# Row maxima of an attention layer from three of six products, two heads at a time in the two halves of TensorE's rows

## The reference

```python
q = qkv[..., :nH * d].reshape(B, S, nH, d)
k = qkv[..., nH * d:nH * d + d]
v = qkv[..., nH * d + d:]
scores = jnp.einsum('bqhd,bkd->bhqk', q, k) * scale
alibi = slopes[:, None, None] * (pos_k - pos_q).astype(jnp.float32)
scores = jnp.where(causal[None, None], scores + alibi[None], NEG_INF)
probs = jax.nn.softmax(scores, axis=-1)
attn = jnp.einsum('bhqk,bkd->bqhd', probs, v).reshape(B, S, H)
return attn @ Wo
```

## Time and profile before

| | |
|---|---|
| Time, median of 3 runs | 1293.03 us (1291.48 to 1293.97) |
| The profiled execution, time | 1289.91 us |
| The profiled execution, span of the trace | 1288.1 us |
| PE busy (matmul) | 1170.8 us, 91% |
| DVE busy | 715.8 us, 56% |
| ACT busy | 583.2 us, 45% |
| Mean granted TensorE clock | 0.977 of full speed |

### The profile page before, as it was taken

One profiled execution on the slowest core, in us unless ns is written; L12 is line 12 of the kernel. 1 busy time (PEld: TensorE's weight loads), 2 busy tenths in 40 slices (PEclk: granted clock), 3 DMA queues, 4 the chain that ended last, 5 costly groups with the idle time before them and its releaser, 6 DMA issues. The chain is left out here.

```text
span 1288.1 us, 16700 instructions
## 1 busy us (share of the span) xinstructions
PE 1170.8 (91%) x6137; PEld 715.2 (56%) x6208; DVE 715.8 (56%) x1374; ACT 583.2 (45%) x1047; POOL 338.5 (26%) x366
## 2 busy tenths in 40 slices
PE   4879999999989999999998799999999999299995
PEld 4535534543543433344535577788788787256663
DVE  4378598688678897788713643331421300655654
ACT  5425456465547677857574443211111111134443
POOL 1214114112220231211034554111211111115554
PEclk9989999999989999999999999999999999699998
DMA  4451502400140420303120222300200100500304
GB/s 157 97 83 55 94 18 42 108 17 18 29 87 1 107 34 18 75 18 67 28 99 26 73 66 87 107 22 1 98 1 1 66 1 1 150 28 5 126 0 130
DMA packets 71567, 72.15 MB, mean 56 GB/s; under 512 B 39826, under 2 KB 45226, under 8 KB 71468
## 3 DMA queue, kind: packets, MB, share of 16 engines
q1 hardware_dynamic: 67284, 60.35, 18.8%
q0 software_dynamic: 3152, 8.63, 2.1%
q10 hardware_dynamic: 1056, 2.16, 0.5%
HBM read 51.86 MB, written 18.87 MB: 55 GB/s over the span
## 5 line engine op out<-in xcount | busy, mean ns | idle before, releaser
L1125 DVE TENSOR_REDUCE mx<-bank 128x1 f32<-128x512 f32 (+2 forms) x576 | 364.6, 684 | 98.5 <-PE bank L1317 54.7
L1048 ACT ACTIVATE PT<-ST 128x512 f32<-128x512 f32 x576 | 311.4, 600 | 106.4 <-PE ST L1393 62.4
L1314 PE MATMUL bank<-KS,QS 125*128 125x512 bf16 (+2 forms) x896 | 204.1, 309 | 12.5 <-DMA QS<-q_scratch 4.2
L1393 PE MATMUL ST<-QS,KS 128*128 128x512 bf16 x527 | 185.0, 383 | 9.1 <-DMA QS<-mparts 3.3
L1407 PE MATMUL PO<-PT,V 128*32 128x512 f32 x1152 | 152.8, 604 | 1.4 <-ACT PT L1048 1.0
L1694 DVE TENSOR_TENSOR f_h<-f_h,f_pair 128x512 f32<-128x512 f32 (+1 forms) x44 | 30.2, 687 | 207.5 <-ACT f_h L1643 207.5
L1314 PEld LDWEIGHTS bank<-KS,QS 125*128 125x128 bf16 x896 | 78.5, 99 | 113.3 <-DVE mx L1125 33.5
L56 PE MATMUL f_pair<-f_xT,gw 128*128 128x512 f32 (+1 forms) x352 | 140.0, 398 | 0.0
L58 PE MATMUL f_pair<-f_xT,gw 128*128 128x512 f32 (+1 forms) x352 | 137.9, 392 | 0.0
L57 PE MATMUL f_pair<-f_xT,gw 128*128 128x512 f32 (+1 forms) x352 | 137.9, 392 | 0.0
L1643 ACT ACTIVATE f_h<-f_pair 128x512 f32<-128x512 f32 (+1 forms) x44 | 26.3, 598 | 218.9 <-PE f_pair L58 218.8
(11 more groups left out here) (208 smaller groups left out, 1806.6 us busy)
## 6 DMA issues: line engine op xcount, KB each, us to landing
QS<-q_scratch SPq DMA_DIRECT2D x96, 128.0 KB
l_x<-x_dram SPq DMA_DIRECT2D x12, 512.0 KB, 4.1
q_scratch<-QP SPq DMA_DIRECT2D x36, 128.0 KB, 1.9
xres<-_attn_hidden_states_dram POOLq DMA_DIRECT2D x16, 256.0 KB, 3.1
x_dram<-xout POOLq DMA_DIRECT2D x16, 256.0 KB, 2.4
xin<-x_dram SPq DMA_DIRECT2D x4, 1024.0 KB, 7.6
f_xsum<-x_dram SPq DMA_DIRECT2D x4, 1024.0 KB, 7.2
x_dram<-f_xsum SPq DMA_DIRECT2D x4, 1024.0 KB, 4.6
```

Source lines behind the costliest of these rows:

```text
L1048: act.activation(PT[:, quad % PT_RING, n % 4, :], ST[:, n % ST_RING, :], ACT.Exp).then_inc(p_done, 1)
L1125: v.tensor_reduce(mx[:, i % 2, z, h:h + m], at(u).rearrange("p (m k) -> p m k", m=m), AX.X, ALU.max).then_inc(bank_free_dve, 1)
L1314: last = pe.matmul(at(u)[:, j * w:(j + 1) * w], QS[0:ROWS1, slot, h + j, :], KS[b][0:ROWS1, k0:k0 + w], start=(j == 0 or not diag), stop=( ...
L1393: last = pe.matmul(dst, KS[b][0:ROWS2, kb * P:(kb + 1) * P], QS[0:ROWS2, slot, h:h + 4, :], start=True, stop=not diag)
```

## The change

Only three of the six products go into the maxima (high with high, high with middle, middle with high). `Q_PART` and `K_PART` are reordered so that these three come first. The 128 rows of `QS` now consist of two halves of 64. For the first 16 heads the upper half holds the first three products, the six position rows and the three rows of the maxima (48 + 6 + 3), and the lower half the other three products; for the last 16 heads the halves are exchanged. So for each batch there are two arrangements of the keys, `KS[b][0]` and `KS[b][1]`, the second copied from the first by two DMAs for each piece (`swap_keys`). The second pass still contracts over all 128 rows.

A unit `p1` now makes two banks: head h in rows 0 to 53 and head h + 16 in rows 64 to 117, by alternate matmuls that write to neighbouring banks. The mask is then added to each bank by a matmul of its own, with the moving operand repeated by a stride of zero. DVE reduces both banks in one instruction of 1024 elements. There are 288 such units. Since a pair must not wrap round the ring, the planner leaves out a bank (`skipped`) where one would. The planner's cost of a unit is 240 ns on PE (218 before, for one bank) and 1130 ns on DVE (690 before, for one bank).

The stack of a block is twelve DMAs of half the size instead of six; the maxima go in by six DMAs instead of three; the position rows and key rows are loaded by more DMAs at the start. `keys_done` is two instructions for a piece instead of one.

```diff
@@ -32,12 +32,16 @@
 PARTS = 3
-Q_PART = (0, 0, 0, 1, 1, 2)
-K_PART = (0, 1, 2, 0, 1, 0)
+
+
+
+Q_PART = (0, 0, 1, 0, 1, 2)
+K_PART = (0, 1, 0, 2, 1, 0)
 SETS = len(Q_PART)
-POS = slice(SETS * HD, SETS * HD + 2 * PARTS)
-ROWS1 = P - PARTS
+ROWS1 = SETS // 2 * HD + 2 * PARTS
 ROWS2 = P
+HALVES = (0, P // 2)
+V_AT = P // 2 - HD
 QSLOTS = 4
 AHEAD = 2
...
@@ -181,7 +185,24 @@
 def maxima_of(i):
-    return [("p1", i, z, h) for z, (_, w, _) in enumerate(segments(BLOCKS[i][1])) for h in range(0, NH, 512 // w)]
+    return [("p1", i, z, h) for z, (_, w, _) in enumerate(segments(BLOCKS[i][1])) for h in range(0, NH // 2, 512 // w)]
+
+
+def banks_of(u):
+
+    return 2 if u[0] == "p1" else 1
+
+
+def skipped(n, count):
+
+    return int(count == 2 and n % RING == RING - 1)
+
+
+def take_banks(taken, u):
+
+    if skipped(len(taken), banks_of(u)):
+        taken.append(taken[len(taken) - RING])
+    taken.extend([u] * banks_of(u))
...
@@ -220,7 +241,7 @@
-    took = {"dt": 400, "dv": 520, "ds": 300, "p1": 218, "tile": 218, "pv": 1060, "xt": 400, "q": 700, "kv": 700, "vt": 400, "mt": 200, "ot": 400, "at": 400, "wo": 700}
+    took = {"dt": 400, "dv": 520, "ds": 300, "p1": 240, "tile": 218, "pv": 1060, "xt": 400, "q": 700, "kv": 700, "vt": 400, "mt": 200, "ot": 400, "at": 400, "wo": 700}
     reads = {"pe": 280, "act": 270, "dve": 270, "pool": 200, "sp": 0}
     free = {"pe": 0, "act": 0, "dve": 0, "pool": 0, "sp": 0}
...
@@ -283,7 +307,7 @@
     def pe_choices():
         out = []
-        dve_load = free["dve"] + sum(690 for j, r in pend["dve"] if r <= free["pe"] + 300)
+        dve_load = free["dve"] + sum(1130 if j[0] == "p1" else 690 for j, r in pend["dve"] if r <= free["pe"] + 300)
         act_load = free["act"] + sum(600 for j, r in pend["act"] if r <= free["pe"] + 300)
         if at["p1"] < len(p1):
...
@@ -478,7 +502,7 @@
                 end["xt", j[1], j[2]] = done
             elif kind == "kv3":
-                end["ks", j[1]] = done
+                sp_issue(("swap", j[1]), done)
             elif kind == "vt":
                 end["v", j[1]] = done
...
@@ -684,15 +708,15 @@
         kvf2 = sb("kvf", [P, 2, HALF])
         kvf = kvf2[:, 0, :]
-        mask = sb("mask", [P, 2, 512], BF16)
+        mask = sb("mask", [P, 2, P], BF16)
         gmask = sb("gmask", [P, 3])
         wo_s = [sb(f"wo{i}", [P, DC, D]) for i in range(2)]
         moments = sb("moments", [P, 4, 2])
         rstd = sb("rstd", [P, 4])
-        kpart = sb("kpart", [SETS * HD, 2, HALF], BF16)
-        krest = sb("krest", [SETS * HD, HALF])
-        KS = [sb(f"KS{b}", [P, S], BF16) for b in range(B)]
+        krest = kvf2[0:V_AT + P // 2, 1, :]
+        kpart = sb("kpart", [V_AT + P // 2, 2, HALF], BF16)
+        KS = [[sb(f"KS{b}{t}", [P, S], BF16) for t in range(2)] for b in range(B)]
         V = [sb(f"V{b}", [P, QB, 32]) for b in range(B)]
         gf = sb("d_gf", [P, DQ_COLS])
...
@@ -775,6 +800,10 @@
             return bank[:, AT[u] % RING, :]
+        def both(u):
+
+            return bank[:, AT[u] % RING:AT[u] % RING + 2, :]
+
         def full(eng, u):
...
@@ -837,20 +867,31 @@
                                  QP[:, part, m, cols_of(k)].rearrange("p (t q) -> p t q", q=P)).then_inc(q_out, 16)
+            def swap_keys(k):
+                b, t, n = PIECES[k]
+                sp.wait_ge(ks_ready, 2 * k + 2)
+                for x in range(2):
+                    sp.dma_start(KS[b][1][HALVES[1 - x]:HALVES[1 - x] + V_AT, t * P:(t + n) * P],
+                                 KS[b][0][HALVES[x]:HALVES[x] + V_AT, t * P:(t + n) * P]).then_inc(ks_swapped, 16)
+
             def stack(i):
                 (b, qb), slot = BLOCKS[i], i % QSLOTS
                 if i >= QSLOTS:
                     sp.wait_ge(st_full, TILE_ENDS[i - QSLOTS + 1])
-                for g, part in enumerate(Q_PART):
-                    sp.dma_start(QS[g * HD:(g + 1) * HD, slot, :, :].rearrange("d (m h) q -> d m (h q)", m=4),
-                                 q_scratch[b, qb, part].rearrange("m d h q -> d m (h q)")).then_inc(qs_in[slot], 16)
+                for t in range(2):
+                    for g, part in enumerate(Q_PART):
+                        r = HALVES[t ^ (g >= SETS // 2)] + g % (SETS // 2) * HD
+                        sp.dma_start(QS[r:r + HD, slot, NH // 2 * t:NH // 2 * (t + 1), :].rearrange("d (m h) q -> d m (h q)", m=2),
+                                     q_scratch[b, qb, part, 2 * t:2 * t + 2].rearrange("m d h q -> d m (h q)")).then_inc(qs_in[slot], 16)
             def stack_max(i):
                 for part, ready in enumerate((m_hi_done, m_mid_done, m_lo_done)):
                     sp.wait_ge(ready, i + 1)
-                    sp.dma_start(QS[ROWS1 + part:ROWS1 + part + 1, slot, :, :], mparts[:, i % 2, part, :]).then_inc(m_in[slot], 16)
+                    for t, r in enumerate(HALVES):
+                        heads = slice(NH // 2 * t, NH // 2 * (t + 1))
+                        sp.dma_start(QS[r + ROWS1 + part:r + ROWS1 + part + 1, slot, heads, :], mparts[heads, i % 2, part, :]).then_inc(m_in[slot], 16)
             load_x(0)
...
@@ -859,16 +900,21 @@
                 sp.dma_start(dst[:], src).then_inc(stack_in, 16)
             for b in range(B):
-                sp.dma_start(KS[b][POS.start:ROWS2, :], krows_d).then_inc(kpos_in, 16)
+                for t in range(2):
+                    for x, r in enumerate(HALVES):
+                        sp.dma_start(KS[b][t][r + V_AT:r + P // 2, :], krows_d[t, x]).then_inc(kpos_in, 16)
             for slot in range(QSLOTS):
                 if slot == 0:
                 else:
                     sp.wait_ge(qs_zero_act, slot)
-                sp.dma_start(QS[POS, slot, :, :], pos_d).then_inc(qs_in[slot], 16)
+                for t, r in enumerate(HALVES):
+                    heads = slice(NH // 2 * t, NH // 2 * (t + 1))
+                    sp.dma_start(QS[r + V_AT:r + ROWS1, slot, heads, :], pos_d[:, heads, :]).then_inc(qs_in[slot], 16)
                 if slot == 0:
                     for m in range(4):
                         q_parts_out(0, m)
+                    swap_keys(0)
                     stack(0)
             for kind, i, *m in ORDER["sp"][1:]:
...
@@ -998,12 +1046,12 @@
                 elif kind == "kv":
                     n = PIECES[u[1]][2] * P
-                    act.activation(kpart[:, 0, 0:n], at(u)[0:SETS * HD, 0:n], ACT.Copy).then_inc(kv_copied, 1)
+                    act.activation(kpart[:, 0, 0:n], at(u)[0:K_ROWS, 0:n], ACT.Copy).then_inc(kv_copied, 1)
                     act.activation(kvf[:, 0:n], at(u)[:, 0:n], ACT.Copy).then_inc(kv_copied, 1)
                 elif kind == "mt":
                     i = u[1]
                     if i >= 2:
-                        act.wait_ge(m_in[(i - 2) % QSLOTS], 16 * PARTS * ((i - 2) // QSLOTS + 1))
+                        act.wait_ge(m_in[(i - 2) % QSLOTS], 32 * PARTS * ((i - 2) // QSLOTS + 1))
                     act.activation(mparts[:, i % 2, 0, :], at(u)[0:NH, 0:P], ACT.Copy).then_inc(m_hi_done, 1)
                 elif kind == "at":
...
@@ -1122,7 +1171,7 @@
                 m = 512 // w
                 full(v, u)
-                v.tensor_reduce(mx[:, i % 2, z, h:h + m], at(u).rearrange("p (m k) -> p m k", m=m), AX.X, ALU.max).then_inc(bank_free_dve, 1)
+                v.tensor_reduce(mx[:, i % 2, z, :].rearrange("p (t h) -> p t h", t=2)[:, :, h:h + m], both(u).rearrange("p t (m k) -> p t m k", m=m), AX.X, ALU.max).then_inc(bank_free_dve, 1)
             def join_max(i):
...
@@ -1187,8 +1236,10 @@
                 b, t, n = PIECES[k]
                 v.wait_ge(k_mid_done, k + 1)
-                v.scalar_tensor_tensor(KS[b][0:SETS * HD, t * P:(t + n) * P], kpart[:, 1, 0:n * P], gmask[0:SETS * HD, 1:2], krest[:, 0:n * P],
-                                       ALU.mult, ALU.add).then_inc(ks_ready, 1)
+                toks = slice(t * P, (t + n) * P)
+                for r in HALVES:
+                    r = slice(r, r + V_AT)
+                    v.scalar_tensor_tensor(KS[b][0][r, toks], kpart[r, 1, 0:n * P], gmask[r, 1:2], krest[r, 0:n * P], ALU.mult, ALU.add).then_inc(ks_ready, 1)
             def max_done(i):
...
@@ -1298,8 +1349,9 @@
             def bank_for(u):
-                if AT[u] >= RING:
-                    freed(pe, BEGUN[AT[u] - RING])
+                for n in range(AT[u], AT[u] + banks_of(u)):
+                    if n >= RING:
+                        freed(pe, BEGUN[n - RING])
             def row_max(u):
...
@@ -1307,15 +1359,17 @@
                 m = 512 // w
                 if u == maxima_of(i)[0]:
-                    pe.wait_ge(qs_in[slot], 16 + 16 * SETS * (i // QSLOTS + 1))
-                    pe.wait_ge(ks_ready, keys_piece(i) + 1)
+                    pe.wait_ge(qs_in[slot], 32 + 32 * SETS * (i // QSLOTS + 1))
+                    pe.wait_ge(ks_swapped, 32 * (keys_piece(i) + 1))
                 bank_for(u)
                 for j in range(m):
```

(58 more changed lines are left out.)

6 lines of the change are left out of this document (3 added, 3 removed).

## The result

The change makes the kernel slower: 1323.59 us (median of 4 runs, 1322.04 to 1326.28) against 1293.5 us for the kernel before measured beside it, a ratio of 1.0243 with a 95% interval of 1.0225 to 1.0261. That is some 30 us. The forecast was 1293 us, with 1281 to 1306 as its own range.

What follows compares the result with a forecast made beforehand. PE's instruction list was taken to bound the attention. PE's list -6, DVE -4, ring +4, first stack +2.6, maxima transfers +4 gave +0.6 us: 1290.5 from the profile, 1293.6 from the median; forecast 1293, range 1281 to 1306.

Steps and rivals of the forecast that it cites:

- the one on the DMAs: SP's queue: twelve DMAs delay the first stack, +2.6 us; key swaps cost nothing; later stacks are two blocks ahead.
- The transfers of the maxima: SP's queue: three more issues of 0.51 us delay a block's first tile by 0.5 us; +4 us, bounds 0 and 8.
- The ring: Four PSUM banks hold two units, not four, so PE waits longer for reductions: +4 us, bounds 0 and 75.
- The rival that named it: PE stands at `bank_for` with all behind it: 1318 us; chance 0.23, shared with a dearer change of mode.
- DVE's gain: Reductions of 1024 elements make DVE 48 us lighter, but DVE waits for PE: -4 us, bounds 0 and -10.
- PE's list: PE's instructions: pairs save 62.2 us, changes of mode add 63.4, pairs beside values save 7: -6 us.
- the rival of fewer changes: PE: pairs mostly stand beside values or each other, so fewer changes of mode: 1268 us, chance 0.20.
- The two rivals that had the pairs gain in full, or not overlap: PE's pairs: no gap at mode changes, 1231 us, chance 0.07; or changes paid and nothing saved, 1355 us, chance 0.06.
- half of 160 units in twos: PE: unmasked pairs in a row save changes of mode; taken as 0, -16 us if half came in twos.
- the first rival: PE: half-row tiles enter and leave without a gap, 62 us go, other terms cancel: 1231 us, chance 0.07.

Runs made afterwards that it cites:

- swaps ahead: The kernel after, with each swap of keys issued ahead of the stacks and maxima directly before it in SP's order: 1304.53 us, ratio 1.0102.
- the kernel with all three repairs: The kernel after, with swaps issued before stacks and maxima, six DMAs for a stack, three for the maxima: 1296.35 us, ratio 1.0052.

## Why the prediction was wrong

**The step that failed** is the one on the DMAs. It said of the swap that it "is queued before it on SP, in time in which SP still waits for the stored queries", "so nothing is taken", and of the stacks that "Later stacks are two blocks ahead". It followed the swap for the first piece, where little was wrong: behind the swap, the first stack was issued from 30.21 on instead of 29.39, 0.8 us later. The 2.6 us for twelve DMAs did not come. By the records of the trace the last of them landed 7.4 us after the first was issued, as with six (37.63 and 36.80), and the first maxima, 1.4 us late at 38.27, waited for VectorE in the end. For the later pieces it took the stacks for work far ahead of its use and forgot what is queued behind them. On the second, third and fifth piece a swap stood behind two stacks of 5.5 to 5.9 us each, once with the transfers of the maxima between them, and PE's order had the maxima next. Nor could the planner see it, which counts 0.6 us of SP for a stack. The term, taken as 0, was 18 us (swaps ahead), with the stalls themselves adding up to 21.4.

**The transfers of the maxima** were the right mechanism at the wrong size: +4 us was taken, with a bound of 8; undoing the six DMAs gave 11 us, of which 6.9 are PE's wait for the maxima. The delay is more than the 0.5 us of the last issue: where the parts are ready, six took SP 3.7 us and three 1.8, and the first two of the three new ones did not vanish in a wait for the next part. The longer stacks are not what made this wait grow: with stacks halved it was still 10.8 us, and with stacks doubled in the kernel before it stayed at 3.0.

**The ring** was a term of the right kind and too small: +4 us taken, 9.6 measured for units of two banks alone, with DVE's pace and the order in it, which no run separates. The rival that named it expected PE to stand at `bank_for`; it does, in stretches in which PE's order holds little but maxima, but it gave only a third of the loss. That its 1318 lies near the measured 1323.6 is luck.

**DVE's gain** of -4 us did not show in the waits of PE, which rose. One instruction for two banks is worth some 3 us where units are of two banks, and its duration was right.

**PE's list** was right in its mechanism and nearly in size. The pairs do overlap, a change of mode costs 0.21 us in and out (0.22 taken, of which 0.01 for a second weight load that no row shows), and the pairs are worth 8.5 or 13.6 us, as the setting goes, where 6 were forecast. In the trace, 81 pairs stand right behind values and 16 right before them, 97 sides where 72 were taken, so the rival of fewer changes does not hold either. The two rivals that had the pairs gain in full, or not overlap, are refuted by the timeline. The rule of the Trainium skill ("TensorEngine Tiling (Array Packing)", Key Properties) that a change of mode drains TensorE agrees with the 0.11 and 0.10 us. The figure of the Trainium skill in "TensorE: Matmul & The Clock Gate", Part 3, that packed matmuls start about 4 ns apart agrees with the 3 to 6 ns between the two of a pair in the trace, and says nothing of the way in and out, by which most of the gain is lost here.

Two sums of the rivals were wrong, without weight for the result: half of 160 units in twos save 40 changes, 8 us and not 16, and in the first rival the other terms do not cancel but add up to 7 us.

The terms do not add up to the 30 us exactly, since they share stalls: 18, 10 and 11 us, each undone alone, gave back 25 us together. The lower clock is part of all of them and was not measured by itself.

## What to carry to other kernels

When a change adds transfers, follow each new one through its queue at every place where it is issued, not only at the first: what stands ahead of it, how long that takes to issue, and which engine has nothing else to do until it lands. Splitting a transfer in two doubles the time for which it holds its queue, and work that was safely ahead becomes an obstacle to a short, urgent transfer behind it. Packing two small matmuls into the array pays most where several packed matmuls follow one another or stand beside work in another mode; a pair alone between full matmuls costs as much as two single ones (0.43 us here), and its larger unit of buffers is a price of its own.

## What the runs showed of the hardware

SP was held as long by a DMA of 64 KB as by one of 128 or 192 KB, about 0.43 us and 0.04 to the next: twelve took 5.46 to 6.96 us to issue in the kernel after, six 2.66 to 3.21 before, and six of 64 to 192 KB 2.66 to 2.94 us in the kernel with all three repairs, one stack of 3.90 aside. So more bytes or partitions in one DMA cost nothing at the issue. The landing was another matter: the first stack took 7.4 us from its first issue to its last landing, in six DMAs and in twelve.

Two matmuls in the two halves of the rows start 3 to 6 ns apart and run at once; the way from the full array into this mode costs 0.10 to 0.11 us and the way back as much. Behind a group of values, a pair starts as soon as a score tile does: 0.998 us after the first of the eight.

A reduction of 1024 elements over two PSUM banks takes 1.22 us, and 1.15 from one to the next in a row; one of 512 over one bank took 0.68.
